# A decoder block on one core: the last step of two inner layer normalizations moves from VectorE to GpSimd, with a new order of all steps

## The chip, the core and the metric

The kernel runs on one core of a Trainium2 chip. A core has TensorE (PE, matrix products and transposes, results in PSUM), VectorE (DVE), ScalarE (ACT), GpSimd (POOL, which reads and writes SBUF only) and SyncE (SP, which here issues all DMAs). Each engine works through its own queue in order and waits at semaphores. The metric is the device time of one execution in microseconds; lower is better.

## What is computed

x is 16 sequences of 256 tokens by 256 channels, float32. Three blocks follow each other, each with a residual and a layer normalization without gain:

```python
def _layernorm(x, axis=-1, eps=1e-05):
    m = jnp.mean(x, axis=axis, keepdims=True)
    v = jnp.var(x, axis=axis, keepdims=True)
    return (x - m) / jnp.sqrt(v + eps)
...
    x = _layernorm(x + _L0_attn_ref(x, ...))                          # recurrent block
    x = _layernorm(x + _L0_xattn_ref(x, ctx_1024, ctx_1024, mask, ...))  # cross attention
    x = _layernorm(x + _L0_ffn_ref(x, k0, k1, k2, s0, s1, s2))        # network
```

The recurrent block quantizes tokens to 8 bits, makes a decay, an input gate and a value, scans them over time, and adds a gated two-layer product. Cross attention has 16 heads of 16 channels with a rotation of queries and keys and a softmax over 256 context tokens. The network has three layers (256 doubled to 512, 1024, 1024, 256) with weights of plus or minus one.

## The kernel before

The kernel goes sequence by sequence. A sequence g has two tiles of 128 tokens (NT = 2), and its work is cut into some 100 named steps in seven stages: weights (once), recurrent, keys, context, queries, scores, values, network. Steps of three to four sequences are in work at once. The order is written as two tables of numbers, TIMES and BEGIN: a step of sequence g on an engine has the key BEGIN[stage][g] + TIMES[step][engine], and each engine issues its steps by rising key (`order`, lines 156 to 160 of the profile's file). The tables set nothing but order; the waits are semaphores. In a table entry the letters P, A, V, G, S stand for PE, ACT, DVE, POOL and SP. The same keys also decide which PSUM buffer an item gets (class Ring): bankA (2 buffers), slotB (2) and bankC (2).

The steps that matter below:

- "down" (VectorE, L1574) adds the last product of the recurrent block to x. "bn" takes mean and variance on VectorE (`moments1`, L1580 and L1583) and 1/rms on GpSimd (`norm1`: L705 adds eps, L706 is the power -0.5). "x1" (VectorE, `normalized`, L1588) subtracts the mean and multiplies by 1/rms, in two instructions of 128x256. "x1T" turns x1 on TensorE (L1088), "q" makes the queries (L1172), "rotq" rotates them (L745 on GpSimd, L1608 and L1613 on VectorE), "qp" splits them in two float16 parts (L1619 on VectorE).
- "kput", "kget", "qput", "qget" on SP write the parts of keys and queries to DRAM and read them back stacked for the scores (L499; L526, L511, L514). "loadx" and "loadc" load x and the context of a sequence two further on (L461, L467). "kp" is the keys' second part (GpSimd, L736).
- "score0" to "score7" (TensorE, L1227) give scores, of which VectorE takes the largest (L1625). "exp" and "pv" are the exponentials and their products with the values. "wo" (TensorE, L1179 into slotB) is the output product; VectorE adds the residual (L1649). "bn2" (`moments2`, `norm2`, the same lines as bn) and "x2" (again L1588) are the second normalization, "x2T" turns x2 on TensorE (L1277), and xl (L1663) is its low part.
- "l0_0" to "l2.3" are the network's products (L1305, L1321, L1337), all on TensorE with ScalarE and VectorE behind them. "sqT" are transposes of the gate's output sg (L1098), "rqT" transposes of the recurrent block's xg (also L1098), "cn" a sum of squares of the context (L1186 on TensorE, L831 on ScalarE).
- "w:h0" to "w:h31" are 32 pieces of four matmuls (L1353) whose results nobody reads; they stand in TensorE's queue while the first sequences fill the engines. "w:down" (L608 to L610), "w:sq" (L616 to L627), "w:wk" and "w:wq" (L638) prepare weights on GpSimd.

Of the kernel before, what the change touches and what calls it, by code (L numbers as in the profile page):

```python
# [12 lines left out]
ALU = mybir.AluOpType  # L13
# [12 lines left out]
G = NB  # L26
# [24 lines left out]
def twice(value):  # L51
# [18 lines left out]
        w:s V-263.918 P-33.33 | w:m V-108.075 A-77.331 P-6.605 | w:a V-73.876 | w:iv V5.493  # L70
        w:g1 A-3.358 P8.562 | w:g2 V3.798 A11.384 P9.22 | w:gate V19.404 | w:down G21.772
        w:bv P24.051 A24.1 | w:bias P25.594 V27.347 | w:h0 P47.419 | w:h1 P102.413 | w:h2 P46.217
        w:h3 P85.865 | w:h4 P23.865 | w:h5 P44.217 | w:h6 P89.958 | w:h7 P74.245 | w:h8 P38.17
        w:h9 P34.502 | w:h10 P36.301 | w:h11 P43.521 | w:h12 P32.429 | w:h13 P85.103 | w:h14 P76.295
        w:h15 P81.068 | w:h16 P77.294 | w:h17 P75.571 | w:h18 P28.426 | w:h19 P30.322 | w:h20 P74.194
        w:h21 P44.13 | w:h22 P29.446 | w:h23 P56.444 | w:h24 P81.824 | w:h25 P27.787 | w:h26 P58.459
        w:h27 P40.021 | w:h28 P64.996 | w:h29 P26.96 | w:h30 P37.959 | w:h31 P60.405
        w:mask V27.902 S27.86 P31.659 | w:sgn V7.473 | w:k0 V40.786 | w:k2 V36.224 | w:k1.0 A30.322
        w:k1.1 A36.129 | w:k1.2 A49.931 | w:k1.3 A65.615 | w:rope G11.429 P11.587 A20.034
        w:bqk P22.429 A22.378 | w:sq A16.526 P22.588 V26.041 G23.673 | w:bs G28.203 A47.636  # L80
        w:tab V34.438 | w:wk G40.558 | w:wq G47.854""",
    "recurrent": """
        loadx S22.409 | scale A6.309 G5.506 V-2.079 | stat1 G14.589 | round V12.582 | xqT P15.494 A16.27
        iv0 P20.273 A21.121 V21.669 | iv1 P23.546 A24.791 V25.263 | a P17.542 A18.25
        aT P22.161 A24.322 | sq A25.854 | ivT P26.013 V30.152 | cum V30.709 | recur V31.238
        rec P33.78 A34.525 V37.039 | max2 V37.214 | stat2 G44.951 | round2 V37.579 | rqT P37.695 A40.634
        gate0 P40.03 A45.689 V47.598 | gate1 P41.923 A46.505 V47.921 | stat3 G58.37 | round3 V48.221
        sqT P51.963 A52.497 | down P55.011 V58.175 | bn V58.199 G68.331 | x1 V61.585""",
    "keys": """
# [1653 lines left out]
```

## Time and profile before

| | us |
|---|---|
| median of 3 runs | 849.92 |
| lowest, highest | 847.07, 851.01 |
| the profiled execution | 846.09 |
| its span, first to last instruction | 844.2 |

| engine | busy us | share of the span | instructions |
|---|---|---|---|
| PE | 786.2 | 93% | 6893 |
| PE weight load | 572.9 | 68% | 6926 |
| DVE | 611.8 | 72% | 1199 |
| ACT | 579.5 | 69% | 960 |
| POOL | 317.9 | 38% | 562 |

The profile is of one execution. The profiler's page gives busy time by engine, the chain of work that ended last, and groups of equal instructions; answers of the trace give busy time by stretch of the span, waits of one engine by whom it waited for, and the instructions of a stretch in order of time. TensorE holds 84% of the chain that ended last, VectorE 8%. DMA moves 40.69 MB at a mean of 48 GB/s. The mean granted clock of TensorE is 0.979 of full speed.

### The profile page before, as it was taken

The page shows a single profiled execution, that of the slowest core. Times are in us where ns is not written, and L with a number is a line of the kernel's source. Part 1 is how long each engine was busy: PE and PEld are TensorE (multiplying, and loading weights), DVE is VectorE, ACT ScalarE, POOL GpSimd, SP SyncE. Part 2 cuts the span into 40 slices and gives each one's busy share as a digit, 9 for nine tenths or more (in the row PEclk, how much of TensorE's full clock was granted, in tenths as well). Part 3 has the DMA queues.
Part 4 walks back from the last instruction along what each step waited for, and adds up shares of the span by engine and source line. Part 5 has one row for each costly group of instructions (what it writes and reads, how often), then busy time and mean ns, then how long its engine had stood idle before and what let it go on. Part 6 is the DMA issues. An engine that isn't in the chain of part 4 may idle for free.

```text
span 844.2 us, 18112 instructions
## 1 busy us (share of the span) xinstructions
PE 786.2 (93%) x6893; PEld 572.9 (68%) x6926; DVE 611.8 (72%) x1199; ACT 579.5 (69%) x960; POOL 317.9 (38%) x562
## 2 busy tenths in 40 slices
PE   1897768999999999999999999999999999999996
PEld 1454326677786868686867768686868777776675
DVE  5754768696978788786969687878879696857242
ACT  6665476959687786869595967778695959563622
POOL 6983225251433423453424343342434251330010
PEclk9999589999999999999999999999999999999998
DMA  9003010203020211111020302111120202020000
GB/s 306 8 26 107 13 33 4 87 2 90 14 82 22 61 42 43 61 37 55 16 86 14 89 14 71 33 58 45 39 64 15 77 14 64 14 64 14 2 13 26
DMA packets 53029, 40.69 MB, mean 48 GB/s; under 512 B 7344, under 2 KB 52432, under 8 KB 52944
## 3 DMA queue, kind: packets, MB, share of 16 engines
q1 hardware_dynamic: 52944, 39.53, 15.5%
q8 instruction: 56, 0.92, 0.4%
q14 instruction: 29, 0.24, 0.1%
HBM read 26.66 MB, written 12.59 MB: 46 GB/s over the span
## 4 chain that ended last, share of the span: by engine, by line
PE 84%; DVE 8%; ACT 4%; issue 2%; POOL 1%; ACTq 0%; DVEq 0%; POOLq 0%
PE bankC L1321 27%; PE bankA L1258 7%; PE bankA L1172 7%; PE bankC L1305 6%; PE bankC L1337 6%; PE bankA L1107 5%; PE slotB L1245 4%; PE slotB L1227 4%; PE slotB L1179 3%; PE bankA L1088 3%; PE bankA L1179 3%; DVE nmax L1625 2%; PE bankC L1353 2%; PE slotB L1277 2%; PE bankA L1098 2%
## 5 line engine op out<-in xcount | busy, mean ns | idle before, releaser
L1321 PE MATMUL bankC<-h0h,w 128*128 128x256 f16 x1024 | 232.4, 273 | 0.5 <-DVE h0l L1669 0.5
L1321 PE MATMUL bankC<-h0l,w 128*128 128x256 f16 x1024 | 231.8, 273 | 0.0
L1625 DVE TENSOR_REDUCE nmax<-slotB 128x4 f32<-128x1024 f32 x128 | 153.9, 1215 | 17.5 <-PE slotB L1227 17.5
L964 ACT ACTIVATE pr<-slotB,cscale 128x1024 f32<-128x1024 f32 x128 | 139.1, 1118 | 10.9 <-PE slotB L1245 10.6
L1321 PEld LDWEIGHTS bankC<-h0h,w 128*128 128x128 f16 x1024 | 100.2, 98 | 28.6 <-issue 14.1
L1321 PEld LDWEIGHTS bankC<-h0l,w 128*128 128x128 f16 x1024 | 100.2, 98 | 15.4
L1258 PE MATMUL bankA<-pr,v_aug 128*32 128x256 f32 x1024 | 69.5, 389 | 0.0
L1669 DVE SCALAR_TENSOR_TENSOR h1l<-bankC,h1h 128x512 f16<-128x512 f32 x64 | 43.5, 679 | 25.8 <-ACT h1h L994 25.6
L1305 PE MATMUL bankC<-xh,w 128*128 128x256 f16 x256 | 58.6, 273 | 1.9 <-DVE h0l L1669 1.1
L745 POOL TENSOR_TENSOR qt<-qb,turn 128x256 f32<-128x256 f32 x32 | 22.7, 730 | 98.8 <-ACT qb L918 98.8
L1337 PE MATMUL bankC<-w,h1h 128*128 128x256 f16 x256 | 59.1, 273 | 0.7 <-DVE h1l L1669 0.6
L1669 DVE SCALAR_TENSOR_TENSOR h0l<-bankC,h0h 128x512 f16<-128x512 f32 x64 | 43.2, 684 | 22.3 <-ACT h0h L994 21.9
L1337 PE MATMUL bankC<-w,h1l 128*128 128x256 f16 x256 | 59.0, 273 | 0.0
L1305 PE MATMUL bankC<-xl,w 128*128 128x256 f16 x256 | 58.4, 273 | 0.0
L705 POOL TENSOR_SCALAR rstd<-mv 128x2 f32<-128x2 f32 x48 | 11.3, 235 | 122.6 <-DVE mv L1583 121.3
L670 POOL TENSOR_SCALAR st<-st 128x2 f32<-128x2 f32 x32 | 6.2, 194 | 135.9 <-ACT junk L885 133.1
L994 ACT ACTIVATE h1h<-bankC 128x512 f16<-128x512 f32 x64 | 37.7, 589 | 26.1 <-PE bankC L1321 26.1
L1245 PE MATMUL slotB<-q_st,k_st 51*128 51x256 f16 x512 | 44.3, 277 | 6.9 <-ACT pr L964 4.5
L1227 PE MATMUL slotB<-k_st,q_st 49*128 49x256 f16 x512 | 47.7, 280 | 2.7 <-DVE nmax L1625 1.4
L994 ACT ACTIVATE h0h<-bankC 128x512 f16<-128x512 f32 x64 | 36.9, 603 | 13.1 <-PE bankC L1305 12.4
L1258 PEld LDWEIGHTS bankA<-pr,v_aug 128*32 128x32 f32 x1024 | 26.9, 110 | 25.1 <-issue 10.9
L848 ACT ACTIVATE sqT<-bankA,cst 128x1024 bf16<-128x1024 f16 x16 | 17.8, 1114 | 37.9 <-PE bankA L1098 37.9
(253 smaller groups left out, 1779.0 us busy)
## 6 DMA issues: line engine op xcount, KB each, us to landing
x<-in_x SPq DMA_DIRECT2D x16, 256.0 KB, 2.9
cT<-in_ctxT SPq DMA_DIRECT2D x16, 256.0 KB, 3.0
scr<-kpart SPq DMA_DIRECT2D x16, 256.0 KB, 2.6
k_st<-scr SPq DMA_DIRECT2D x32, 128.0 KB
scr<-qpart SPq DMA_DIRECT2D x16, 256.0 KB, 2.3
q_st<-scr SPq DMA_DIRECT2D x32, 128.0 KB, 2.7
out<-x SPq DMA_DIRECT2D x16, 256.0 KB, 2.1
k_st<-scr SPq DMA_DIRECT2D x32, 64.0 KB
```

Of the source, the lines that this page charges most:

```text
L964: act.activation(pr[i % 2][:, c, :, :].rearrange("p h s -> p (h s)"), slotB[ringB.slot(g, name)][:, :], ACT.Exp, scale=cscale[:, g:g + 1])\
L994: act.activation(flat(dst[:, 2 * m:2 * m + 2, :]), bankC[ringC.slot(g, item)][:, :], ACT.Relu)\
L1172: ins = pe.matmul(bankA[ringA.slot(g, name)][:, e * T:(e + 1) * T], w[:, c, e * P:(e + 1) * P], xT[:, c, :], start=c == 0, stop=c == CT - 1)
L1179: ins = pe.matmul(bank[:, n * D:(n + 1) * D], xT[:, c, n * P:(n + 1) * P], w[:, c, :], start=c == 0, stop=c == CT - 1)
L1227: ins = pe.matmul(slotB[ringB.slot(g, f"score{un}")][:, j * T:(j + 1) * T], q_st[g % 2][rows_, h, n * P:(n + 1) * P], k_st[g % 2][rows_, h ...
L1245: ins = pe.matmul(slotB[ringB.slot(g, name)][:, j * T:(j + 1) * T], k_st[g % 2][rows_, h, c * P:(c + 1) * P], q_st[g % 2][rows_, h, :], st ...
L1258: ins = pe.matmul(bank[j * VW:(j + 1) * VW, half_:half_ + T], v_aug[g % 2][:, c, i * HG + j, :], pr[i % 2][:, c, j, :], start=c == 0, stop ...
L1305: ins = pe.matmul(bankC[ringC.slot(g, name)][:, e * T:(e + 1) * T], w_0[:, c, (2 * m + e) * P:(2 * m + e + 1) * P], a[:, c, :], start=i == ...
L1321: ins = pe.matmul(bankC[ringC.slot(g, name)][:, e * T:(e + 1) * T], w_1[:, i // 2, (2 * m + e) * P:(2 * m + e + 1) * P], (h0h, h0l)[i % 2] ...
L1337: ins = pe.matmul(bankC[ringC.slot(g, "l2.0")][:, n * D:(n + 1) * D], (h1h, h1l)[i % 2][:, i // 2, n * P:(n + 1) * P], w_2[:, i // 2, :], ...
L1625: dve.tensor_reduce(nmax[:, 0:H * NT].rearrange("p (a q b n) -> p q n a b", a=2, q=NHG, b=2)[:, hg, n], slotB[ringB.slot(g, name)][:, :].r ...
L1669: dve.scalar_tensor_tensor(flat(lo[:, two, :]), bankC[ringC.slot(g, item)][:, :], 0.0, flat(hi[:, two, :]), ALU.max, ALU.subtract).then_in ...
```

## The change

`normalized`, the two tensor_scalar instructions of x1 and of x2, goes from VectorE's block to GpSimd's. The instruction is the same, with the mean and 1/rms as per-partition factors from SBUF. The waits are the same too: for the mean and variance, and for 1/rms, which is now GpSimd's own. Both tables are replaced by new ones, so all engines have a new order. ScalarE's squares of the context wait for their own of the sequence before.

```diff
-        bn2 V141.116 G149.518 | x2 V145.874""",
+        bn2 V144.525 G142.741 | x2 G145.798""",
...
-    "values": [3.061, 49.863, 97.46, 145.457, 193.061, 240.531, 287.745, 335.036,
+    "values": [-1.755, 45.711, 93.45, 141.792, 189.334, 236.16, 285.011, 333.182,
...
+            def normalized(dst, src, mv_, rstd_):
+                for n in range(NT):
+                    ins = pool.tensor_scalar(dst[:, n, :], src[:, n, :], mv_[:, n, 0:1], rstd_[:, n:n + 1],
+                                             ALU.subtract, ALU.mult)
+                return ins
+
+            def x1_(g):
+                pool.wait_ge(*mv_s.at(g))
+                pool.wait_ge(*rstd_s.at(g))
+                normalized(x1[g % 2], x[g % 2], mv[g % 2], rstd[g % 2]).then_inc(x1_s.sem, 1)
+
+            def x2_(g):
+                pool.wait_ge(*mv2_s.at(g))
+                pool.wait_ge(*rstd2_s.at(g))
+                normalized(x2[g % 2], x2[g % 2], mv2[g % 2], rstd2[g % 2]).then_inc(x2_s.sem, 1)
...
+                if g >= 1:
+                    act.wait_ge(*csq_s.at(g - 1))
                 act.activation(junk[:, 2].rearrange("p n d -> p (n d)"), flat(cT[g % 2]), ACT.Square,
                                accum_out=csq[:, g:g + 1]).then_inc(csq_s.sem, 1)
...
-            def normalized(dst, src, mv_, rstd_):
-                for n in range(NT):
-                    ins = dve.tensor_scalar(dst[:, n, :], src[:, n, :], mv_[:, n, 0:1], rstd_[:, n:n + 1],
-                                            ALU.subtract, ALU.mult)
-                return ins
```

GpSimd's queue around the second normalization of a steady sequence, before. The last row of the rotation of the keys is kt<-kt, rstd is 1/rms, st are the scales of the next sequence's tokens.

```order
L730 TENSOR_TENSOR kt<-kt 128x512
L702 TENSOR_SCALAR st<-st,wstat 128x2
L705 TENSOR_SCALAR rstd<-mv 128x2
L706 TENSOR_TENSOR rstd<-rstd,half 128x2
L670 TENSOR_SCALAR st<-st 128x2
```

The same place now (line numbers of the new file):

```order
L747 TENSOR_TENSOR kt<-kt 128x512
L706 TENSOR_SCALAR rstd<-mv 128x2
L707 TENSOR_TENSOR rstd<-rstd,half 128x2
L715 TENSOR_SCALAR x<-x,mv,rstd 128x256 x2
L671 TENSOR_SCALAR st<-st 128x2
```

The normalization of x2 stands between its 1/rms and the next sequence's scales; the small scale L702 (now L703) has gone ahead of the keys' rotation.

TensorE around the product with w_o of sequence 6, before. k_st,q_st are scores, csq the sum of squares of the context, sg the gate's output, w,h1h the first matmul of the network's last layer.

```order
L1321 MATMUL bankC<-h0l,w 128x256
L1227 MATMUL slotB<-k_st,q_st 128x256 x4
L1186 MATMUL bankA<-csq,ones 128x1
L1179 MATMUL slotB<-w_o,oT 128x256 x4
L1098 MATMUL bankA<-ident_h,sg 128x128 x8
L1337 MATMUL bankC<-w,h1h 128x256
```

The same place now:

```order
L1340 MATMUL bankC<-h0l,w 128x256
L1117 MATMUL bankA<-ident_h,sg 128x128 x8
L1246 MATMUL slotB<-k_st,q_st 128x256 x4
L1198 MATMUL slotB<-w_o,oT 128x256 x4
L1356 MATMUL bankC<-w,h1h 128x256
```

The transposes of sg have gone from behind the product with w_o to ahead of it. From there to the transposes of x2, in both, stand three of the four quarters of the last layer (24 matmuls), two scores and the down product; in some sequences now also the sum of squares.

SP's queue at the beginning, after the keys of sequence 0 are read, before. scr is the DRAM buffer, kpart and qpart the two parts of keys and queries, k_st and q_st their stacked form.

```order
L499 DMA scr<-kpart 128x4x256
L467 DMA cT<-in_ctxT 128x2x256
L499 DMA scr<-qpart 128x4x256
L526 DMA k_st<-mscr 1x8x256 x2
L511 DMA k_st<-scr 16x4x512
L514 DMA k_st<-scr 32x4x512
L511 DMA k_st<-scr 16x4x512
L514 DMA k_st<-scr 32x4x512
L511 DMA q_st<-scr 16x4x512
L514 DMA q_st<-scr 32x4x512
```

And now:

```order
L462 DMA x<-in_x 128x2x256
L500 DMA scr<-qpart 128x4x256
L512 DMA q_st<-scr 16x4x512
L515 DMA q_st<-scr 32x4x512
L512 DMA q_st<-scr 16x4x512
L515 DMA q_st<-scr 32x4x512
L500 DMA scr<-kpart 128x4x256
L468 DMA cT<-in_ctxT 128x2x256
L527 DMA k_st<-mscr 1x8x256 x2
```

The queries of sequence 0 are written and read ahead of everything of sequence 1.

## Rows read from the trace of the kernel before

**Rows 1.** Stretch, its length, busy PE, PEld, DVE, ACT, POOL, clock, DMA, GB/s.

```profile
50.00:100.00 50.00, 40.78 (x215) 21.32 (x216) 32.59 (x67) 26.69 (x47) 24.13 (x44) 0.85 0.20 56
100.00:148.00 48.00, 35.65 (x273) 22.82 (x275) 34.00 (x66) 33.20 (x55) 16.25 (x28) 0.87 0.09 22
337.00:385.00 48.00, 47.71 (x441) 36.11 (x441) 36.68 (x73) 36.59 (x60) 22.86 (x40) 1.00 0.18 53
770.00:844.00 74.00, 63.13 (x578) 49.10 (x575) 28.71 (x56) 25.10 (x38) 5.98 (x16) 0.97 0.04 12
```

**Rows 2.** What TensorE waited for, 148 to 770 us: total, times, longest.

```profile
PE bankA L1107 <- issue: 2.1, 13, 0.2
PE slotB L1277 <- DVE x L1588: 0.2, 1, 0.2
```

**Rows 3.** Groups by line: count | busy us, mean ns | idle before, releaser.

```profile
L1588 DVE TENSOR_SCALAR x<-x,mv,rstd 128x256 f32<-128x256 f32 x64 | 24.5, 424 | 2.9 <-POOL rstd L706 1.8
L745 POOL TENSOR_TENSOR qt<-qb,turn 128x256 f32<-128x256 f32 x32 | 22.7, 730 | 98.8 <-ACT qb L918 98.8
L757 POOL TENSOR_SCALAR nb<-mv,rstd 128x1 f32<-128x1 f32 x32 | 9.5, 310 | 1.6
L609 POOL TENSOR_SCALAR h1l<-h1l 128x1024 f32<-128x1024 f32 x1 | 4.0, 3964 | 0.1
L608 POOL TENSOR_SCALAR h1l<-h1l,wstat 128x1024 f32<-128x1024 f32 x1 | 1.7, 1707 | 0.9 <-DVE wstat L1409 0.9
```

**Rows 4.** TensorE in order of time, sequence 6: start us, us, instruction.

```profile
408.80 1.97 PE L1179 MATMUL slotB<-w_o,oT 128*128 128x256 f32 x8
410.61 0.61 PE L1098 MATMUL bankA<-ident_h,sg 128*128 128x128 f16 x8
411.05 0.27 PE L1337 MATMUL bankC<-w,h1h 128*128 128x256 f16 x1
...
415.20 0.60 PE L1277 MATMUL slotB<-ident,x 128*128 128x128 f32 x4
```

**Rows 5.** VectorE and GpSimd at the same place, in order of time.

```profile
410.91 0.69 DVE L1649 TENSOR_TENSOR x<-slotB,x 128x512 f32<-128x512 f32 x1 [0.29 <-PE slotB L1179]
...
412.58 1.19 DVE L1625 TENSOR_REDUCE nmax<-slotB 128x4 f32<-128x1024 f32 x1
413.85 0.73 DVE L1588 TENSOR_SCALAR x<-x,mv,rstd 128x256 f32<-128x256 f32 x2
...
413.03 0.71 POOL L706 TENSOR_TENSOR rstd<-rstd,half 128x2 f32<-128x2 f32 x1
```

**Rows 6.** SP's DMA issues at the beginning, in order of time.

```profile
75.58 0.47 SPq L499 DMA_DIRECT2D scr<-qpart  x1
76.10 1.39 SPq L526 DMA_DIRECT2D k_st<-mscr  x2
...
80.15 0.54 SPq L511 DMA_DIRECT2D q_st<-scr  x1
```

**Rows 7.** VectorE, then TensorE, between 71 and 103 us, in order of time.

```profile
71.35 0.69 DVE L1619 TENSOR_TENSOR qpart<-qt,qpart 128x512 f16<-128x512 f32 x1 [0.90 <-ACT qpart L935]
...
99.47 0.74 DVE L1588 TENSOR_SCALAR x<-x,mv,rstd 128x256 f32<-128x256 f32 x2
...
101.94 0.48 DVE L1513 SCALAR_TENSOR_TENSOR iv<-bankA,st,iv 128x256 f32<-128x256 f32 x1 [1.73 <-ACT iv L857]
...
83.48 0.40 PE L1098 MATMUL bankA<-ident_h,xg 128*128 128x128 f16 x4 [3.10 <-DVE xg L1499]
```

**Rows 8.** The chain that ended last, in the drain: start us, us, what.

```profile
809.32 0.75 DVE x L1588 x2
...
810.11 0.66 PE slotB L1277 x4
...
810.80 2.78 PE bankC L1337 x24
```

**Rows 9.** GpSimd near 44 us, in order of time.

```profile
43.95 2.40 POOL L697 TENSOR_SCALAR st<-st,wstat 128x2 f32<-128x2 f32 x1
```

More of the change, by code:

```diff
@@ L69 @@
     "weights": """
[L70 to L74, printed above, removed]
@@ L81 @@
-        w:tab V34.438 | w:wk G40.558 | w:wq G47.854""",
-    "recurrent": """
[L83 to L88, printed above, removed]
+        w:s V-109.416 P-235.292 | w:m V-61.916 A-78.863 P-78.498 | w:a V-33.708 | w:iv V9.274
@@ new lines @@
+        w:g1 A-20.166 P-57.232 | w:g2 V-33.035 A5.482 P-5.466 | w:gate V20.22 | w:down G24.601
+        w:bv P19.33 A29.628 | w:bias P30.309 V43.841 | w:h0 P86.176 | w:h1 P42.529 | w:h2 P71.696
+        w:h3 P72.228 | w:h4 P29.45 | w:h5 P39.1 | w:h6 P36.843 | w:h7 P75.767 | w:h8 P71.011
+        w:h9 P44.031 | w:h10 P81.473 | w:h11 P58.194 | w:h12 P41.746 | w:h13 P35.068 | w:h14 P81.04
+        w:h15 P49.524 | w:h16 P86.587 | w:h17 P54.019 | w:h18 P49.461 | w:h19 P33.736 | w:h20 P81.618
+        w:h21 P39.935 | w:h22 P32.305 | w:h23 P38.892 | w:h24 P88.476 | w:h25 P48.414 | w:h26 P71.773
@@ new lines @@
+        w:h27 P93.192 | w:h28 P69.776 | w:h29 P32.562 | w:h30 P32.61 | w:h31 P63.951
+        w:mask V22.638 S42.463 P26.498 | w:sgn V11.755 | w:k0 V37.502 | w:k2 V74.564 | w:k1.0 A33.81
+        w:k1.1 A47.355 | w:k1.2 A98.011 | w:k1.3 A99.028 | w:rope G4.933 P10.909 A14.006
+        w:bqk P26.04 A29.332 | w:sq A5.604 P16.277 V22.299 G24.8 | w:bs G32.51 A35.654 | w:tab V35.314
+        w:wk G22.834 | w:wq G47.921""",
+    "recurrent": """
+        loadx S52.825 | scale A3.518 G-1.668 V0.017 | stat1 G12.263 | round V12.57 | xqT P14.059 A14.612
+        iv0 P19.623 A19.908 V21.353 | iv1 P22.03 A23.191 V23.895 | a P16.39 A17.565 | aT P20.863 A22.314
+        sq A25.878 | ivT P25.256 V29.306 | cum V29.606 | recur V29.943 | rec P34.129 A36.098 V36.042
+        max2 V37.096 | stat2 G34.33 | round2 V37.336 | rqT P38.192 A41.491
+        gate0 P41.178 A45.398 V49.319 | gate1 P41.957 A45.736 V49.761 | stat3 G46.936 | round3 V50.067
+        sqT P49.434 A51.1 | down P53.771 V57.662 | bn V58.595 G63.374 | x1 G64.517""",
@@ L132 @@
-    "network": [3.16, 50.852, 98.492, 145.952, 193.36, 240.625, 288.135, 335.797,
-                382.121, 430.659, 478.667, 527.011, 574.337, 621.953, 671.467, 716.257],
+    "recurrent": [-0.66, 49.614, 88.531, 135.892, 183.529, 231.781, 279.794, 326.268,
+                  374.815, 423.008, 470.766, 518.245, 566.007, 614.489, 662.016, 710.243],
+    "keys": [0.628, 28.788, 99.364, 146.077, 195.191, 243.312, 290.794, 337.939,
+             386.297, 433.097, 481.691, 529.815, 577.668, 625.606, 674.002, 722.055],
@@ new lines @@
+    "context": [1.505, 27.51, 90.702, 120.442, 138.776, 231.519, 264.476, 310.208,
+                378.17, 407.226, 469.991, 496.331, 543.829, 595.083, 646.446, 694.711],
+    "queries": [1.463, 44.937, 86.165, 133.897, 181.381, 229.846, 276.615, 324.739,
+                373.507, 421.406, 467.726, 515.832, 564.918, 612.561, 660.717, 709.875],
+    "scores": [1.294, 37.045, 84.208, 131.925, 180.273, 227.706, 274.78, 323.033,
+               371.059, 418.831, 466.142, 514.178, 562.874, 610.456, 658.332, 706.214],
```

75 lines of the change are left out of this document (27 added, 48 removed).

## The prediction, made before the changed kernel ran

> **What bounds the kernel now.** I read the busy time by stretch first. In the steady part, 337 to 385 us, TensorE is busy 47.71 of 48 us, while VectorE has 36.68, ScalarE 36.59 and GpSimd 22.86 [rows 1]. So there the period is TensorE's own work, and a microsecond taken from VectorE is worth nothing by itself. The waits say the same from the other side: from 148 to 770 us TensorE waited 2.1 us in 13 pieces of at most 0.2 us and 0.2 us once for x2 [rows 2]. No reordering can gain more than these 2.3 us in 622. What is left lies at the two ends: from 50 to 148 us TensorE is idle 9.22 + 12.35 = 21.6 us (and more before), of the last 74 it is idle 10.9, and its granted clock is 0.85 and 0.87 of full in the two stretches from 50 to 148 us [rows 1]. The sum below asks three things: does the new place of x2 make TensorE wait in each sequence, and what does the new order do at the beginning and at the end.
>
> **What moves.** 64 tensor_scalar instructions of 128x256 leave VectorE (424 ns each, 24.5 us in all) and go to GpSimd [rows 3]. VectorE's gain is worth nothing in the steady part, by the paragraph above. GpSimd has the room (22.86 us of 48 busy [rows 1]). What counts is latency, and it counts where TensorE comes close behind.
>
> **The price of one normalization on GpSimd.** The trace has no 128x256 tensor_scalar of this form there. The nearest is L608: two per-partition factors from SBUF, add and multiply, f32 to f32, 1024 elements, 1707 ns. The same form with one element (L757) takes 310 ns. A line through the two gives 310 + 255 x 1397/1023 = 658 ns for 256 elements, and two in a row, overlapping by about 0.1 us, 1.2 us. Bounds: not less than two one-element ones with their overlap (0.5 us); a two-input operation of the same 256 elements (L745) takes 730 ns, a pair 1.4 us; and L609, a tensor_scalar with add and max, takes 3964 ns for 1024, which by the same line is 1.2 us each and 2.4 us the pair [rows 3]. I take 1.2 us, since L608 has the very form, and keep 0.5 and 2.4.
>
> **x2 in the steady part (the main cost).** Take sequence 6. The product with w_o starts on TensorE at 408.80, VectorE adds the residual at 410.91 and takes the mean and variance, GpSimd has 1/rms at 413.03 + 0.71 = 413.74, VectorE starts to normalize at 413.85 and ends at 414.58 [rows 4, 5]. TensorE turns x2 at 415.20 [rows 4]: a slack of 0.62 us. The spacing repeats in every steady sequence but number 8, whose piece of work between is one shorter. In the new order TensorE has less between these two points, as the transposes of sg (410.61 to 411.05, 0.44 us [rows 4]) now stand ahead of the product. So TensorE is ready for x2 at 415.20 - 0.44 = 414.76. On GpSimd x2 needs no hop to VectorE, but waits for its own power (0.1 us): 413.74 + 0.1 + 1.2 = 415.04, and 0.05 to TensorE (as from 809.32 + 0.75 = 810.07 to 810.11 in the drain [rows 8], where TensorE really waited), so 415.09. That is a stall of 0.33 us. It is paid in full, as nothing on TensorE is elastic. In sequences 1 to 13 it comes 13 times, in six of them the small sum of squares of the context (0.1 us) now stands in between: 13 x 0.33 - 0.6 = +3.7 us. With the pair at 0.5 there is no stall; with 1.4 it is 0.53, +6.3; with 2.4 it is 1.53, +19. The old order's own wait for x2 (0.2 us, sequence 8 [rows 2]) goes: -0.2.
>
> The Trainium skill bears on this price (GPSIMD Engine Reference, Engine selection): it keeps elementwise work on VectorE, calls GpSimd about two times slower for two inputs, and one input roughly line rate. The two-input rows agree with it. What one input at line rate would mean is a rival below.
>
> **x1** has cover. In the new order TensorE has about 1 us more work between the down product and the transposes of x1, and VectorE reaches its mean and variance earlier since x2 is off its queue. What is queued behind x1 on GpSimd is the second part of the keys (L736) and the query's rotation (L745); the DMA of the keys then leaves some 1 us later, but the scores of that sequence stand behind the rest of the query path and most of a network stage. What stands behind x2 there is the scale of the next sequence's tokens (L670 on), again with microseconds to spare. Cost 0. The added wait in context_squares is for ScalarE's own earlier square, long done. Cost 0.
>
> **The beginning.** Query parts of sequence 0 are ready at 71.35 + 0.69 = 72.04, but SP's queue holds their DMA behind the next keys' write and the load of the next context; it goes at 75.58. Then the keys of sequence 1 (from 76.10, four microseconds of issuing) stand ahead of the queries' own read, which starts at 80.15 [rows 6]. In the new order both query steps of sequence 0 stand ahead of everything of sequence 1: up to 75.58 - 72.04 = 3.5 and 80.15 - 76.10 = 4.05 us less, except some 2 us that the read then has to wait for the write; 5.5 to 6 us off the arrival. But the first scores stand in both orders behind the transposes rqT of sequence 1 at 83.48 on TensorE [rows 7], which hang on that sequence's recurrence and not on the queries. So I take 1 us of the 6 there. In the score phase the new order puts the decay projection of sequence 2 ahead of two scores, and the input projection follows at once; in the old one VectorE waited 1.73 us for that gate at 101.94 with a maximum queued behind it, and did x1 just before, at 99.47, 0.74 us [rows 7]. I take 1.5 us there, and 0.5 us for x2 of sequence 0, which stood behind two maxima. Together -3 us. Against it: the reordering of w_k (3 us on GpSimd) ahead of w_down delays the floor value and VectorE with it by some 2 us, but w_k is then no longer waited for by the first key product; I count these as even. Range -7 to +6, the upper end for the clock (below).
>
> **The end.** The last sequence's x2 is turned at 810.11 in the chain; then TensorE has 2.78 us of layer 2 before it goes on at 813.58 [rows 8]. In the new order one of these three pieces (0.93 us) stands ahead of x2's transposes. The chain is later by 1.2 + 0.1 - 0.1 - 0.74 = 0.46 us, and 0.93 us of work has moved ahead of it: about -0.5. For sequence 14 the same swap is even.
>
> **Sum**, against the profiled execution (846.09 us: 844.2 of span and 1.9 around it): +3.7 - 0.2 - 3 - 0.5 = 0.0. This execution lies 3.8 us under the median of the three runs (849.92), so I put the sum on the median: **850 us**.
>
> **Rivals.**
> A (my forecast, 0.42): stalls and savings nearly cancel, 846 to 854.
> B, 0.27, faster: x2 is cheap on GpSimd or the beginning gains its full 6 us. Pair at most 0.9 us: the stall is 0.03, the steady part costs nothing, and the beginning's -3 to -6 stands: 843 to 846. For it: a two-operand tensor_scalar reads one tensor, so it should be under L745's 0.73, and L608 [rows 3] ran beside VectorE's own work on SBUF, which may have stretched it. By the Trainium skill's line-rate rule (same section) a 256-element pass would add about 0.22 us, an estimate from its 1.2 GHz, to L757's 310 ns: a pair of 0.95, a stall under 0.1 and about 846; no run yet shows it.
> C, 0.13, slower: x2 costs more than the cover. A pair of 1.9 gives 1.03 x 13 = +13, 860; 2.4 gives +19. It decides from a pair above 1.4 us. A way to get there is blocking: at 43.95 a 128x2 tensor_scalar (L697) took 2.40 us [rows 9], where L757's of one element take 0.31 [rows 3]; VectorE ran a long tensor_tensor over SBUF beside it. Against it: what VectorE does while x2 runs is a maximum over PSUM (from 412.58 [rows 5], and another behind it). The Trainium skill (GPSIMD Engine Reference, Key points) says that the two share their SBUF interfaces and collide when a VectorE instruction has two SBUF inputs; by that rule, the row at 43.95 agrees, and x2 beside a PSUM maximum would be spared.
> D, 0.18, slower: the beginning loses. The clock is granted in two levels, 1.2 and 2.4 GHz; its mean of 0.85 from 50 to 100 us [rows 1] means about 30% of the time at the lower, and TensorE paused 3.10 us before 83.48 there [rows 7]. Another order of the filling matmuls (all 32 remain) can lengthen this: 20 us more at half clock with TensorE busy some 60% would cost 6 us: 856. The same mechanism can shorten it, which is part of B.
> That the change does not do what it says is excluded: the instructions stand on the other engine.
>
> **Range and chances.** 842 to 859: it holds A, nearly all of B and D, and leaves out C's far part. About what a measurement can tell here is 0.5%, 4.2 us. Faster by more than that: B, 0.27. Within: 0.43, A and a little of D. Slower: C and the rest of D, 0.30.
>
> **What would show it.** Right: TensorE's waits list x2 (the turned x) about 13 times with 0.2 to 0.4 us each, the GpSimd pair takes 1.1 to 1.3 us, the query read of sequence 0 is issued near 74 us, and the transposes of x2 of sequence 0 come 3 us earlier than now. Wrong: a pair under 0.9 or above 1.5 us, a wait at another place of the steady part (queries or xl), or a beginning that moves by more than 5 us either way.

## The result: 889.3 us, slower by 4.6%

The changed kernel took 889.26 us (median of 4 runs, 888.68 to 889.42) against 850.12 (847.07 to 851.01) of the kernel before: ratio 1.0462, 95% interval 1.0443 to 1.0482. The prediction said 850, with 859 as its upper end. The profiled execution has a span of 886.9 us, 42.7 over the 844.2 shown of before; about 3.8 of these are the profiled execution of before, which lay under its own median.

The busy time by stretch, with the columns of [rows 1]:

```profile
50.00:100.00 50.00, 41.84 (x218) 22.23 (x221) 28.41 (x56) 30.01 (x48) 27.77 (x42) 0.91 0.19 57
100.00:148.00 48.00, 32.22 (x233) 19.02 (x234) 32.13 (x61) 28.73 (x48) 19.52 (x32) 0.78 0.07 20
337.00:385.00 48.00, 45.81 (x422) 34.40 (x422) 35.23 (x69) 33.88 (x56) 21.79 (x37) 1.00 0.15 46
```

In the steady part TensorE was busy 47.71 of 48 us; now it is 45.81 at the same full clock. The time is lost where the prediction said that nothing is elastic. What TensorE waited for from 148 to 800 us (total, times, longest), answering to [rows 2]:

```profile
PE slotB L1296 <- POOL x L715: 18.8, 13, 1.5
PE bankA L1107 <- POOL x L715: 9.5, 12, 1.7
PE bankC L1340 <- DVE h0l L1672: 3.9, 13, 0.3
PE bankC L1324 <- DVE h0l L1672: 0.4, 1, 0.4
```

L1296 turns x2, L1107 turns x1 (among others), L715 is the normalization on GpSimd. 28.3 us wait for the moved instructions, and 3.9 for the low part h0l of the network's first layer, which was no steady wait before. The groups of GpSimd that answer to [rows 3]:

```profile
L715 POOL TENSOR_SCALAR x<-x,mv,rstd 128x256 f32<-128x256 f32 x64 | 78.2, 1229 | 5.7 <-POOL rstd L707 5.7
L610 POOL TENSOR_SCALAR h1l<-h1l 128x1024 f32<-128x1024 f32 x1 | 4.0, 3966 | 0.1
L609 POOL TENSOR_SCALAR h1l<-h1l,wstat 128x1024 f32<-128x1024 f32 x1 | 1.6, 1610 | 0.0
```

One 128x256 instruction took 1229 ns, not the 658 of the prediction. One steady sequence in order of time (start us, us, instruction), TensorE's two rows last; it answers to [rows 4, 5]:

```profile
431.67 0.75 DVE L1599 BATCH_NORM_STATS2 bn<-x 128x6 f32<-128x256 f32 x2
432.45 0.25 DVE L1602 BATCH_NORM_AGGREGATE mv<-bn 128x2 f32<-128x6 f32 x2
...
433.07 0.71 POOL L707 TENSOR_TENSOR rstd<-rstd,half 128x2 f32<-128x2 f32 x1
433.97 2.44 POOL L715 TENSOR_SCALAR x<-x,mv,rstd 128x256 f32<-128x256 f32 x2 [0.18 <-POOL rstd L707]
436.49 0.19 POOL L671 TENSOR_SCALAR st<-st 128x2 f32<-128x2 f32 x1
...
438.75 0.81 POOL L707 TENSOR_TENSOR rstd<-rstd,half 128x2 f32<-128x2 f32 x1
439.74 2.45 POOL L715 TENSOR_SCALAR x<-x,mv,rstd 128x256 f32<-128x256 f32 x2 [0.18 <-POOL rstd L707]
...
436.46 0.66 PE L1296 MATMUL slotB<-ident,x 128*128 128x128 f32 x4 [1.39 <-POOL x L715]
442.24 0.66 PE L1107 MATMUL bankA<-ident,x 128*128 128x128 f32 x4 [0.45 <-POOL x L715]
```

The pair takes 2.44 us behind 0.18 us of waiting for its own power, and TensorE stands idle 1.39 us for x2 and 0.45 for x1. The difference of the spans, cut at the first and the last turning of x2: up to the first (139.06 before, 145.85 now) +6.8, from there to the last (810.11 before, 853.9 now) +37.0, behind it -1.1.

### The profile page after: what moved, and what is told of

Its sections match the earlier page's. It is cut to its first block, busy times and chain, and to the rows that moved or that the text cites. A ratio compares the mean times of both kernels' runs of the same rounds, so it can differ in the third digit from the quotient of the medians.

```text
span 886.9 us, 18127 instructions
## 1 busy us (share of the span) xinstructions
PE 788.7 (89%) x6893; PEld 577.9 (65%) x6926; DVE 591.3 (67%) x1135; ACT 576.8 (65%) x960; POOL 385.2 (43%) x626
## 4 chain that ended last, share of the span: by engine, by line
PE 64%; POOL 15%; DVE 9%; ACT 5%; issue 5%; SPq 1%; DMA 0%; POOLq 0%; ACTq 0%; DVEq 0%
PE bankC L1340 24%; POOL x L715 7%; PE bankA L1277 7%; PE bankA L1191 6%; PE slotB L1264 4%; PE bankA L1126 3%; PE slotB L1198 3%; PE slotB L1246 3%; POOL rstd L707 3%; PE bankA L1107 3%; PE bankC L1324 2%; ACT qb L937 2%; DVE bn L1599 2%; PE slotB L1288 1%; DVE h0l L1672 1%
## 5 line engine op out<-in xcount | busy, mean ns | idle before, releaser
L706 POOL TENSOR_SCALAR rstd<-mv 128x2 f32<-128x2 f32 x48 | 9.3, 193 | 167.3 <-DVE mv L1602 166.1
L715 POOL TENSOR_SCALAR x<-x,mv,rstd 128x256 f32<-128x256 f32 x64 | 78.2, 1229 | 5.7 <-POOL rstd L707 5.7
L1007 ACT ACTIVATE xh<-slotB 128x512 f16<-128x512 f32 x16 | 9.6, 597 | 106.0 <-PE slotB L1296 106.0
L1246 PE MATMUL slotB<-k_st,q_st 49*128 49x256 f16 x512 | 43.2, 274 | 5.9 <-DVE nmax L1633 2.7
```

What stands on the lines that cost most here:

```text
L715: ins = pool.tensor_scalar(dst[:, n, :], src[:, n, :], mv_[:, n, 0:1], rstd_[:, n:n + 1], ALU.subtract, ALU.mult)
L1246: ins = pe.matmul(slotB[ringB.slot(g, f"score{un}")][:, j * T:(j + 1) * T], q_st[g % 2][rows_, h, n * P:(n + 1) * P], k_st[g % 2][rows_, h ...
```

## What sets the price: the form of the instruction

Three theories could explain 1229 ns: the form (F), VectorE beside it (N), or a straight line drawn wrongly from 1024 to 256 elements (S). A fourth (O) blamed the new order. The run "forms" times the forms on GpSimd, each once in one execution, at the end of the kernel of before, when VectorE has ended (its last instruction ends at 841.26 us, the first of these starts at 842.90):

```diff
+            src, dst, m, r = kt1[:, 0, :], kt2[:, 0, :], mv[1][:, 0, 0:1], rstd[1][:, 0:1]
+            own.settle(pool.tensor_scalar(dst, src, m, r, ALU.subtract, ALU.mult))
+            own.settle(pool.tensor_scalar(dst, src, m, r, ALU.add, ALU.mult))
+            own.settle(pool.tensor_scalar(dst, src, r, m, ALU.mult, ALU.add))
+            own.settle(pool.tensor_scalar(dst, src, r, m, ALU.mult, ALU.subtract))
+            own.settle(pool.tensor_scalar(dst, src, 0.5, 2.0, ALU.subtract, ALU.mult))
+            own.settle(pool.tensor_scalar(dst, src, 0.5, 2.0, ALU.add, ALU.mult))
+            own.settle(pool.tensor_scalar(dst, src, m, None, ALU.subtract))
+            own.settle(pool.tensor_scalar(dst, src, m, None, ALU.add))
+            own.settle(pool.tensor_scalar(dst, src, r, None, ALU.mult))
+            own.settle(pool.tensor_scalar(dst, src, 0.5, 2.0, ALU.add, ALU.max))
+            own.settle(pool.tensor_scalar(flat(kt2), flat(kt1), m, r, ALU.subtract, ALU.mult))
+            own.settle(pool.tensor_scalar(flat(kt2), flat(kt1), m, r, ALU.add, ALU.mult))
+            own.settle(pool.tensor_scalar(dst[:, 0:1], src[:, 0:1], m, r, ALU.subtract, ALU.mult))
+            own.settle(pool.tensor_scalar(dst[:, 0:1], src[:, 0:1], m, r, ALU.add, ALU.mult))
+            own.settle(pool.tensor_tensor(dst, src, kt1[:, 1, :], ALU.subtract))
```

The first of these instructions is L771, and each has the next number; kt1, kt2 are spare by then.

> The kernel of before with fifteen extra GpSimd instructions at the end of its queue, one after the other, each waited for by itself, all reading and writing spare buffers; nobody waits for them. They measure what one 128x256 tensor_scalar costs in the forms subtract-multiply (the form of the change), add-multiply, multiply-add, multiply-subtract, a single operation, constants in place of per-partition factors, add-max, the same at 512 and at 1 element, and one two-input subtract. In the changed kernel the subtract-multiply took 1229 ns each. Theory F (form: a subtract, like the max of L609, takes GpSimd a slower way of 3.7 to 3.9 ns an element, an add with a multiply a faster one of 1.4): subtract-multiply 1200 to 1260 ns here too, add-multiply and multiply-add 620 to 700, add-max 1200 to 1300, subtract-multiply at 512 about 2200, add-multiply at 512 about 1000, both at one element about 310. Theory N (neighbours: VectorE's use of SBUF stretches the instruction): here, with VectorE nearly idle, subtract-multiply and add-multiply both near 660. Theory S (size: my straight line from 1024 elements to 256 was wrong whatever the operation, so that a short instruction carries a fixed part of some 900 ns): both near 1230 at 256. The time of the kernel says nothing: the extra work may stand beside or behind its last steps, up to 15 us more.

Its groups (mean ns in the last number before the second bar):

```profile
L771 POOL TENSOR_SCALAR kt<-kt,mv,rstd 128x256 f32<-128x256 f32 x1 | 1.2, 1233 | 0.0
L772 POOL TENSOR_SCALAR kt<-kt,mv,rstd 128x256 f32<-128x256 f32 x1 | 0.5, 547 | 0.1
L773 POOL TENSOR_SCALAR kt<-kt,rstd,mv 128x256 f32<-128x256 f32 x1 | 0.6, 554 | 0.1
L774 POOL TENSOR_SCALAR kt<-kt,rstd,mv 128x256 f32<-128x256 f32 x1 | 1.2, 1228 | 0.1
L775 POOL TENSOR_SCALAR kt<-kt 128x256 f32<-128x256 f32 x1 | 1.1, 1081 | 0.1
L776 POOL TENSOR_SCALAR kt<-kt 128x256 f32<-128x256 f32 x1 | 0.4, 403 | 0.1
L777 POOL TENSOR_SCALAR kt<-kt,mv 128x256 f32<-128x256 f32 x1 | 0.9, 926 | 0.1
L779 POOL TENSOR_SCALAR kt<-kt,rstd 128x256 f32<-128x256 f32 x1 | 0.9, 927 | 0.1
L780 POOL TENSOR_SCALAR kt<-kt 128x256 f32<-128x256 f32 x1 | 1.1, 1081 | 0.1
L781 POOL TENSOR_SCALAR kt<-kt,mv,rstd 128x512 f32<-128x512 f32 x1 | 2.1, 2076 | 0.1
L782 POOL TENSOR_SCALAR kt<-kt,mv,rstd 128x512 f32<-128x512 f32 x1 | 0.8, 765 | 0.1
L783 POOL TENSOR_SCALAR kt<-kt,mv,rstd 128x1 f32<-128x1 f32 x1 | 0.4, 399 | 0.1
L784 POOL TENSOR_SCALAR kt<-kt,mv,rstd 128x1 f32<-128x1 f32 x1 | 0.3, 341 | 0.1
L785 POOL TENSOR_TENSOR kt<-kt 128x256 f32<-128x256 f32 x1 | 0.7, 725 | 0.1
```

Form it is. Subtract-multiply takes 1233 ns with nothing beside it, as in the kernel (1229), so N falls; add-multiply takes 547 at the same size, so S falls. Each element more costs (2076 - 1233)/256 = 3.29 ns with a subtract and (765 - 547)/256 = 0.85 ns with an add. The Trainium skill (GPSIMD Engine Reference, Engine selection) calls one input roughly line rate; at the 1.2 GHz that its Specifications give, that would be an estimate of 0.83 ns, which the add meets and the subtract misses by four times. Theory F held in its order of costs, but several of its numbers missed: add-multiply took 547 ns (expected 620 to 700) and 765 at 512 elements (about 1000), add-max 1081 (1200 to 1300), the two forms of one element 399 and 341 (about 310). Two things I had put no number on: a single operation (926) is dearer than an add with a multiply, and the two-input subtract (725) is cheaper than the one-input subtract-multiply (1233).

In the kernel itself the one word was changed; the mean is then added where it should be subtracted:

```diff
-                                             ALU.subtract, ALU.mult)
+                                             ALU.add, ALU.mult)
```

> The changed kernel with one word changed: the normalization on GpSimd adds the mean where it subtracted it, so its output is not the reference's; order, waits, sizes and buffers are the same. Theory F (the form sets the price): each instruction falls from 1229 to about 660 ns, the pair from 2.44 to 1.2 to 1.3 us. The stalls at the turned x2 fall by 1.2 of their 1.5 us to some 0.3 in 13 sequences, those at the turned x1 by more (two pairs stand in that row on GpSimd, 2.4 us less against a stall of 0.5 to 1.7) to nothing: 889.3 - 13 x 1.2 - 13.7 = 860 at most stalls left, 850 to 856 expected. Theories N and S: pair and time unchanged, 887 to 891. Theory O (the new order itself is to blame, with the pair only as a bystander): pair shorter but the time still above 870.

It took 853.42 us (6 runs, 852.33 to 854.39; ratio 1.0060, 1.0042 to 1.0078). 35.8 of the 39.1 us hang on that word (34.2 by the two ratios, each against its own runs of the kernel before), and the order, the waits and the engine are the same:

```profile
L715 POOL TENSOR_SCALAR x<-x,mv,rstd 128x256 f32<-128x256 f32 x64 | 34.8, 552 | 5.6 <-POOL rstd L707 5.6
```

Written with the right result, the negated mean is made on VectorE:

```diff
+                dve.wait_ge(*mv_s.at(g))
+                dve.tensor_scalar(less[g % 2][:, :], mv[g % 2][:, :, 0], -1.0, None, ALU.mult).then_inc(less_s.sem, 1)
...
-                    ins = pool.tensor_scalar(dst[:, n, :], src[:, n, :], mv_[:, n, 0:1], rstd_[:, n:n + 1],
-                                             ALU.subtract, ALU.mult)
+                    ins = pool.tensor_scalar(dst[:, n, :], src[:, n, :], less_[:, n:n + 1], rstd_[:, n:n + 1],
+                                             ALU.add, ALU.mult)
```

> The changed kernel with the same result, but the normalization on GpSimd written as an addition of the negated mean and a multiplication, the form that took 547 ns in the run of forms. VectorE makes the negated mean in one small instruction of 128x2 behind each mean and variance, beside GpSimd's own 0.9 us for 1/rms. Theory F (the form is the whole price): the pair on GpSimd 1.1 us, time as with the added mean, 852 to 856 (that kernel: 853.4). If the small instruction is not hidden (it delays VectorE's next step, 32 times 0.1 to 0.2 us, on a VectorE that is no bound): up to 858.

853.01 us (10 runs, 852.09 to 855.31; ratio 1.0043, 1.0025 to 1.0062). VectorE's 32 small instructions of some 0.2 us cost nothing that can be told.

## How x1 and x2 share it

```diff
-                normalized(x1[g % 2], x[g % 2], mv[g % 2], rstd[g % 2]).then_inc(x1_s.sem, 1)
+                normalized(x1[g % 2], x[g % 2], mv[g % 2], rstd[g % 2], ALU.subtract).then_inc(x1_s.sem, 1)
...
-                normalized(x2[g % 2], x2[g % 2], mv2[g % 2], rstd2[g % 2]).then_inc(x2_s.sem, 1)
+                normalized(x2[g % 2], x2[g % 2], mv2[g % 2], rstd2[g % 2], ALU.add).then_inc(x2_s.sem, 1)
```

That is x1_dear; x2_dear has the two words exchanged. Each adds one of the two means, so neither output is the reference's.

> The changed kernel with x1 in its own form (subtract, multiply: 1229 ns) and x2 with the mean added in place of subtracted (552 ns), so the output is not the reference's. With both cheap, x1 of sequence 8 ends at 422.47 + 1.09 = 423.56 and TensorE turns it at 424.44, a cover of 0.9 us. Subtracting makes it end 1.36 us later: a stall of 0.5 us, 13 times 6.5 us, and about 1 at the beginning: 859 to 863. If the cost of x1 in the changed kernel came only from the dear x2 ahead of it on GpSimd: 853 to 856, no wait at the turned x1.

> The reverse: x2 subtracts (1229 ns), x1 adds the mean. With both cheap TensorE already comes 0.0 to 0.2 us ahead of x2, so all of the 1.36 us is stall: 13 times 1.36 = 17.7, and 1.4 each for the first and the last sequence: 871 to 875. TensorE is then itself later at x1 by 1.36, so no wait for x1 is left. The two kernels together must give the changed kernel's 36 us above the cheap one (889.3 - 853.4): if the costs simply add, x1_dear and x2_dear stand 6 to 9 and 18 to 21 above 853.4, 24 to 30 in all, and the 6 to 12 that are missing are what the two cost one another in GpSimd's queue (x1 behind x2).

x1_dear took 867.09 (866.07 to 867.58), x2_dear 876.25 (875.21 to 877.23). TensorE's waits for x1 in the first and for x2 in the second, from 148 to 800 us:

```profile
PE bankA L1107 <- POOL x L715: 10.6, 14, 1.7
```

```profile
PE slotB L1296 <- POOL x L715: 18.8, 13, 1.5
```

Above the 853.42 of the kernel with both cheap they stand +13.7 and +22.8, together 36.5, against 35.8 of the changed kernel. So the costs add, and the interaction of 6 to 12 us that I had expected in GpSimd's queue isn't there. Both kernels lie above what I expected (859 to 863 and 871 to 875), x1_dear by 4 us at least. x1 was dearer than worked out: 0.76 us each in place of 0.5, and in x1_dear x2 of sequence 0 is turned at 145.38 us, against 140.48 with both cheap. So 4.9 us fall in the beginning: there TensorE waits 1.55 us for x1 at 68.34 us and 2.86 us at 106.64. With both cheap it waits at the same two places 0.31 us for a part of the keys and 2.10 us for the gate's iv, so these waits explain 2.0 of the 4.9 us; the rest isn't followed up.

## The order by itself

The old order with both normalizations on GpSimd right behind their 1/rms, first in the dear form, then in the cheap one:

```diff
+    if engine == "POOL":
+        return ("bn" if step == "x1" else "bn2", g)
...
+    if engine == 'POOL':
+        for step in ('x1', 'x2'):
+            for g in range(G):
+                out.insert(out.index(behind(step, g, engine)) + 1, (step, g))
```

> The kernel of before with its own tables, and both normalizations on GpSimd, each right behind its own 1/rms in GpSimd's queue; nothing else moves. With a pair of 2.44 us and 0.18 us of waiting for 1/rms: x2 of sequence 6 would be ready at 413.74 + 0.18 + 2.44 + 0.05 = 416.41 against 415.20, a stall of 1.2 us, 13 to 15 times: +16 to +18. The x1 has a stall only if its own cover is less than 1.7 us more than it was; in the changed kernel TensorE had about 1 us more there and still waited 13.7 us in all, so in the old order the wait at x1 should be larger, 1 us or more each: +13 to +25. Together 880 to 893. If the new order had been worth anything as cover, this kernel is slower than the changed one (above 889); if it cost something, it is faster. Under theory O it stays under 865.

> The order of the kernel before, with both normalizations on GpSimd right behind their 1/rms, in the cheap form (negated mean added). It separates the new order from the new engine. With a pair of 1.1 us x2 of sequence 6 is ready at 413.74 + 0.18 + 1.09 + 0.05 = 415.06, against 415.20 where TensorE comes: no stall; x1 had 14.7 us of waits in 13 pieces with the dear form, 1.13 each, and is 1.35 us quicker now, with another 1.35 from the x2 ahead of it: no stall. Theory N1 (what is left above the kernel before, 853.4 against 849.0, is the new order's): 846 to 850, no wait for x in the steady part. Theory N2 (it is GpSimd's latency, whatever the order): 852 to 856, with waits for x of 0.1 to 0.4 us in each sequence.

Dear: 889.06 us (887.05 to 889.98; ratio 1.0479, 1.0451 to 1.0508), the changed kernel's time. Cheap: 849.72 us (12 runs, 847.29 to 851.75; ratio 1.0004, 0.9990 to 1.0019), the time of the kernel before. The waits for the moved steps from 148 to 800 us, dear and then cheap:

```profile
PE slotB L1306 <- POOL x L727: 14.5, 13, 1.9
PE bankA L1117 <- POOL x L727: 10.3, 11, 1.8
```

```profile
PE bankA L1120 <- POOL x L730: 1.6, 4, 0.5
PE slotB L1309 <- POOL x L730: 0.7, 2, 0.6
```

So the change of engine costs nothing with the cheap form, and gains nothing: what leaves VectorE was off the path. The new order costs 853.0 - 849.8 = 3.2 us with the cheap form and nothing that can be told with the dear one (889.3 and 889.1). There it waits longer for x2 (18.8 against 14.5 us) and less for x1 (9.5 against 10.3). Both times lie where they were expected, but in the dear kernel the waits are smaller than worked out: 14.5 us for x2 (16 to 18 expected) and 10.3 for x1 (13 to 25). Between the first and the last turned x2 it needs 37.4 us more than the kernel before, and its waits for x1 and x2 in that stretch are 28.4 (24.8 of them in the list above, which ends at 800 us). From 148 to 400 us its TensorE was busy 242.28 us at a granted clock of 0.99, that of the changed kernel 239.01 at 1.00; so part of the loss stands in the trace as slower work and not as waits. The low clock stands in two pieces, 0.84 from 148 to 156 us and 0.79 from 532 to 540, where the kernel before has 1.00 in both; just ahead of them TensorE had waited for x2, 1.69 us (to 144.15) and 1.93 us (to 532.08). That is an estimate of 8 x 0.16 + 8 x 0.21 = 3 us; at least 6 stay open.

The reverse, the new tables with both normalizations back on VectorE, was run at two places of x1:

```diff
+    if step == "x1":
+        return ("bn", 0) if g == 0 else ("score6", 0) if g == 1 else ("max", g - 1)
+    return ("score7", 1) if g == 0 else ("bn2", 15) if g == 15 else ("score6", g + 1)
...
-        return ("bn", 0) if g == 0 else ("score6", 0) if g == 1 else ("max", g - 1)
+        return ("bn", 0) if g == 0 else ("score6", 0) if g == 1 else ("l2.3", g - 3) if g > 3 else ("max", g - 1)
```

> The changed kernel's tables, but both normalizations back on VectorE, each put at the place among VectorE's steps where the kernel before has it (one or two steps away where the neighbours have changed). If the price on GpSimd is the whole cause (theories F, N and S alike): TensorE's waits for x2 and x1 vanish but for what the order itself costs. The new order takes 0.44 us of TensorE's cover ahead of x2, against a slack of 0.62, so no stall: 846 to 853. Theory O: 870 to 890, with the waits still there. If the beginning has gained the 3 us that the prediction gave it, the time is below that of before, near 847; if not, 850.

> The new order with both normalizations on VectorE again, x1 now placed behind the last layer's sum of sequence g-3 (l2.3) instead of behind the largest scores of g-1. In the run with the other place (873.7), x1 (two instructions, 0.9 us) and its wait for 1/rms stood ahead of that sum, which frees the PSUM buffer that the first layer's product waits for: TensorE waited 9.7 us there, 1.1 each. Theory P (my placing is what cost the 24 us, the new order none of it): those waits go, 855 to 862, with waits of 0.3 to 0.9 us for x1 itself left, since x1 is now 0.8 us later. Theory Q (the new order leaves VectorE no good place for x1, because it lets VectorE take the largest scores before the sum): 866 to 875, with the waits moved to the turned x1.

873.74 us (871.82 to 874.36) at the first place, 864.40 (861.62 to 865.78) at the second. The first expectation, 846 to 853, missed by 20; the time is in theory O's range, but its waits for x are not there. The second time lies between theory P (855 to 862) and theory Q (866 to 875) and decides for neither. The wait behind the first miss, from 148 to 800 us, first and second place (L1690 is l2.3, the sum that frees the buffer of the first layer):

```profile
PE bankC L1321 <- DVE x L1690: 9.7, 9, 1.7
```

```profile
PE bankC L1321 <- DVE x L1690: 1.3, 6, 0.3
```

The second place removes it and 9.3 us with it, and 14.6 stay, 5.4 of them ahead of the first turned x2. How much of that is the order and how much my two places isn't separated. So these two runs don't show what the new order alone is worth with VectorE.

## Where the new order's 3 us may lie

In the cheap kernel TensorE waits for h0l; before there was no such steady wait:

```profile
PE bankC L1343 <- DVE h0l L1679: 3.9, 13, 0.3
PE slotB L1299 <- POOL x L718: 2.0, 7, 1.0
```

The query product q (1.9 us) stands ahead of l0_3 in the new order, so less work lies between l0_3 and the matmul that reads its low part. Four kernels put steps back, the first one two steps and each further one a step more (per engine: the step, True for ahead and False for behind, of which step, of a sequence so much further on). They are mend_l0, mend_both, mend_three and mend_four; what the expectations call three moves are the four of mend_three:

```diff
+MOVES = {'ACT': [('l0_1', True, 'x1T', 2)], 'PE': [('l0_3', True, 'q', 2)]}
...
+MOVES = {'ACT': [('l0_1', True, 'x1T', 2)], 'PE': [('l0_3', True, 'q', 2), ('sqT', False, 'wo', -2)]}
...
+MOVES = {'ACT': [('l0_1', True, 'x1T', 2), ('l0_3', True, 'q', 2)], 'PE': [('l0_3', True, 'q', 2), ('sqT', False, 'wo', -2)]}
...
+MOVES = {'ACT': [('l0_1', True, 'x1T', 2), ('l0_3', True, 'q', 2)], 'PE': [('l0_3', True, 'q', 2), ('sqT', False, 'wo', -2)], 'DVE': [('iv0', True, 'rotq', -1)]}
```

> The kernel of the new order with the cheap form (853.0), with two moves per sequence back to how the kernel before has it: on ScalarE the copy of the network's l0_1 ahead of the copy of the turned x1, and on TensorE l0_3 ahead of the query product q. In the new order q (1.9 us) and the copy of x1 stand ahead of them, and TensorE waits 0.30 us for the low part of l0_3 in 13 sequences (3.9 us in the steady part, 4.3 in all); the kernel before has no such wait. Theory O1 (this exchange is what the new order costs): the wait goes, 853.0 - 3.9 = 849, about the kernel before. Theory O2 (it only moves, to the buffer that l0_3 needs or to the first piece of the next layer): 852 to 855, with a new wait at l0_3.

> The same, and on TensorE the transposes of sg behind the product with w_o again, which gives x2 0.44 us more cover (TensorE waited for x2 2.0 us in 7 pieces of the steady part and 1.9 us for one at the start). Theory O1: 849 - 2 = 847, no wait left in the steady part above 0.5 us. If the down product (which needs sg turned, copied by ScalarE, 0.6 us) then comes too late: a new wait there, and no gain over the kernel with one mend.

mend_l0 took 865.68 us (median; ratio 1.0185, 1.0165 to 1.0205), mend_both 859.25 (858.35 to 860.29). Both expectations failed: the wait grew from 3.9 to 15.2 us, in both kernels (the line is of mend_l0):

```profile
PE bankC L1354 <- DVE h0l L1690: 15.2, 13, 1.2
```

The cause stands in ScalarE's queue of mend_l0:

```profile
436.05 1.02 ACT L951 ACTIVATE qb<-bankA,bs,pre 128x256 f32<-128x256 f32 x2 [2.07 <-PE bankA L1205]
436.96 0.59 ACT L1027 ACTIVATE h0h<-bankC 128x512 f16<-128x512 f32 x1
...
437.59 0.69 DVE L1690 SCALAR_TENSOR_TENSOR h0l<-bankC,h0h 128x512 f16<-128x512 f32 x1 [2.88 <-ACT h0h L1027]
...
438.43 0.27 PE L1354 MATMUL bankC<-h0h,w 128*128 128x256 f16 x1 [1.17 <-DVE h0l L1690]
```

ScalarE waits 2.07 us for q with the copy of l0_3 behind it. The sqT move took x2's waits from 2.0 us in 7 pieces to 1.0 in one, as expected. But mend_both is 6.4 us under mend_l0, while the waits listed from 148 to 800 us are as large as before (18.1 us in mend_l0, 18.3 in mend_both). What fell is the busy time of TensorE with the same number of matmuls, by 5.3 us (mend_l0, then mend_both):

```profile
PE 787.3 (91%) x6893; PEld 577.6 (67%) x6926; DVE 594.9 (69%) x1167; ACT 576.8 (67%) x960; POOL 341.7 (40%) x626
PE 782.0 (91%) x6893; PEld 575.5 (67%) x6926; DVE 594.9 (69%) x1167; ACT 577.5 (67%) x960; POOL 341.7 (40%) x626
```

So the place of the sg transposes is worth more than the cover for x2, and no run shows why.

> The kernel with both mends (859.3) and one move more: on ScalarE the copy of the network's l0_3 ahead of the copy of q too. In the last run TensorE made l0_3 by 0.9 us earlier, but ScalarE had the copy of q (1.02 us) in its queue ahead of the copy of l0_3 and waited 2.07 us for q with l0_3 done behind it: so the low part of l0_3 started at 434.57 instead of near 432, and TensorE waited 1.17 us for it, 13 times, 15.2 us. Theory O3 (this blocked queue is all that is wrong with the mend): the copy of l0_3 starts 2.7 us earlier, the wait of 1.17 us goes in all 13 sequences, 859.3 - 15.2 = 844, and with 1 or 2 us of new small waits 845 to 848, under the kernel before. Theory O2 (the new order has no room for these steps at any place; the wait comes back at the query's path, which is now 0.6 us later, or at the input gate behind it): 850 to 856.

> The kernel with three moves (851.3, waits for the input gate's iv 3.5 us in 13 sequences) and a fourth: on VectorE the input gate's first part ahead of the rotation of the queries, as the kernel before has it. VectorE now waited 0.69 us for GpSimd's half of the rotation with the gate behind it; TensorE then 0.27 us for the gate's sum. Theory O3 (the 3 to 4 us that the new order costs with the cheap form are a few blocked queues in the query path, and nothing else): the wait goes and none comes, 851.3 - 3.5 = 847.8, that is 847 to 849, not to be told from the kernel before. Theory O2 (the new order shifts the wait once more, to the query parts or the scores): 850.5 to 852.

mend_three took 851.34 (12 runs, 849.48 to 851.70; ratio 1.0023, 1.0010 to 1.0036), mend_four 876.11 (875.09 to 879.49). Their largest waits of the steady part:

```profile
PE bankA L1140 <- DVE iv L1546: 3.5, 13, 0.3
```

```profile
PE bankA L1121 <- DVE qt L1632: 28.3, 13, 2.2
```

With mend_three the steady wait for h0l is gone and the input gate's iv takes its place, since VectorE's rotation of the queries stands ahead of it. The 851.34 us lie in theory O2's range. Put iv first, and the rotation frees the PSUM buffer of q too late: TensorE has q ahead of iv0 in the new order, and with two buffers the transposes of ya (L1121) take the one that q leaves. The wait moves on, as O2 said, but at 876.11 us it is some 25 us dearer than either theory allowed (852 at most). What the new order's 3 us are isn't shown. The place of q ahead of l0_3 and iv0, which three engines' queues and a ring of two buffers hold together, makes the listed waits; the place of sqT costs about twice the 3 us in the pair mend_l0 and mend_both, and was never put back by itself in the cheap kernel. None of the four returns beats the kernel before, and none of the versions here is faster than it.

## Why the prediction was wrong, step by step

- TensorE bounds the steady part, VectorE's relief is worth nothing: right. With the cheap form in the old order 64 instructions left VectorE, 32 small ones came, and the ratio was 1.0004.
- The price of a pair, 1.2 us: this step failed. "L608 has the very form" was not true: it adds and multiplies, the change subtracts and multiplies, and on GpSimd that is 1229 against 552 ns. For the form of L608 the number was good (1.1 us). The right value, 2.44, was my far end, from L609's add and max [rows 3]; I chose between ends two times apart by the count of operands, when the rows differed in the operation. And L609 stood there to say that the operation matters. That 1.2 came near 1.1 was partly luck: the line was drawn from a 1024-element row that lies off the slope measured from 256 to 512. I also overlooked tensor_scalar rows of just 128x256 on GpSimd in the trace of before. They have one operation and another access pattern, but at 985 to 1507 ns each they speak for a pair near 2 us or more, not 1.2:

```profile
L638 POOL TENSOR_SCALAR w_k<-kt 128x256 f32<-128x256 f32 x2 | 3.0, 1507 | 0.0
L638 POOL TENSOR_SCALAR w_q<-qt 128x256 f32<-128x256 f32 x2 | 2.7, 1348 | 0.0
L597 POOL TENSOR_SCALAR kt<-rope 128x256 f32<-128x256 f32 x2 | 1.9, 985 | 3.5 <-DMA rope<-in_rope 3.5
```

- x2 with a pair of 2.4, "1.53, +19": right. 18.8 us in the steady part, 13 pieces.
- x1 "has cover. Cost 0": held for the pair of 1.1 us (0.5 us in two pieces with the cheap form), failed at the end of the range. I carried 2.4 us through x2 and not through x1, which had 0.6 us to spare: +13.7 us. That is why even rival C stopped at +19.
- The beginning, -3: failed by some 5 us with the cheap form. The query read of sequence 0 went from 80.15 [rows 6] to 78.46 us, not to 74. And the recurrent path of sequence 0, whose loss and gain by w_k ahead of w_down I counted as even, is later (no run separates what in the order does it): x1 of sequence 0 starts at 66.52 in place of 61.41 and the transposes of sequence 1, on which the first scores hang, at 87.14 in place of 83.48 [rows 7]. The score phase gave 1.9 of these 3.7 back; x2 is turned 1.8 us later than before. The dear form brings it to 6.8. The three rows are of the kernel with the negated mean:

```profile
78.46 0.55 SPq L515 DMA_DIRECT2D q_st<-scr  x1
66.52 1.10 POOL L718 TENSOR_SCALAR x<-x,less,rstd 128x256 f32<-128x256 f32 x2 [0.19 <-POOL rstd L710]
87.14 0.40 PE L1120 MATMUL bankA<-ident_h,xg 128*128 128x128 f16 x4 [2.24 <-DVE xg L1521]
```

  The execution with the added mean, in the same order, has them some 2 us earlier (76.37, 64.53 and 85.04), so about 2 us of such a difference is one execution against another; its x2 is turned 1.4 us later than before.
- The end, -0.5: the direction was right (-1.1). Before's own wait for x2, -0.2, didn't go: with the cheap form TensorE waits 2.0 us for x2 in 7 pieces. Both are too small to matter.
- h0l, 3.9 us, was not in the sum at all. I looked at the work between the producers and consumers of x1 and x2 alone, where a new order shortens every such distance.
- Rival C had the mechanism and the price, at 0.13, and the range left its far part out. Its supposed way, blocking by VectorE, was wrong: 1229 ns beside VectorE, 1233 without.
- Rival B fell with the pair. Rival D: the beginning did lose, but its way, the clock, isn't seen. With the cheap form the granted clock was 0.90 and 0.89 in the two stretches from 50 to 148 us, before 0.85 and 0.87 [rows 1]; with the dear form 0.91 and 0.78.

The profiled executions alone would give 7.8 us for the new order with the cheap form; the medians give 3.2. The difference is the quick execution profiled of before.

## To carry to other kernels

Price a moved instruction by a row with the same operations in the same order, not only the same operands and type; where the trace has none, two rows that differ by a factor say that the operation is unknown, and the dear one counts. Carry each end of such a price through every step that uses it, not through the tightest alone. On GpSimd write x minus mean as x plus the negated mean: 2.2 times as quick here, for one 128x2 instruction on VectorE.

## What was not expected of the hardware

On GpSimd, f32 from SBUF, 128x256: add and multiply with per-partition factors 547 ns, with constants 403; two operations with a subtract among them 1081 to 1233; add and max 1081; one operation alone 926 to 931, be it add, subtract or multiply; a subtract of two inputs 725. An instruction that reads what GpSimd's own power has just written waited 0.18 us for it, not 0.1. That an add-multiply of 1024 elements takes 1607 to 1714 ns, where the step from 256 to 512 gives 765 + 512 x 0.85 = 1200, stays open.
